# Layer 0's scores and maxima in two row tiles of TensorE, in a two-layer gated cross-attention kernel

## The chip, the cores and the metric

One NeuronCore of a Trainium2 chip runs the whole program. The metric is the device time of one execution in microseconds (us).

The engines are TensorE (PE in the profile; PEld is its weight load), VectorE (DVE), ScalarE (ACT), GpSimd (POOL) and SyncE (SP). Here every DMA is issued by SP, from one queue in the order of the program.

## The reference

Sixteen batches, each of 56 query rows and 1,500 context rows of width 128, go through two layers. A layer is a gated cross-attention (16 heads of 8) and a gated feed-forward with 8 experts, of which each row uses 2.

```python
x = x + tanh(g_xattn[0]) * xattn0(layernorm(x), ctx, ctx, ...)        # no mask
x = x + tanh(g_ffn[0])   * moe0(layernorm(x), ...)                     # E=8, F=512, gelu
x = x + tanh(g_xattn[1]) * xattn1(layernorm(x), ctx, ctx, mask, ...)   # mask on the context rows
x = x + tanh(g_ffn[1])   * moe1(layernorm(x), ...)                     # E=8, F=64, and a shared expert
# xattn: softmax(q k^T / sqrt(8)) v for each head, then the output projection
```

## The kernel before

**Steps.** Work goes by steps `s`. Step `s` has the maxima of batch `n = s` (0 to 15 are layer 0, 16 to 31 are layer 1), the scores and exponentials of the batch before, and the key projection of the batch after. The feed-forward of two batches at a time follows some steps behind: an odd step ends the attention of a pair and begins its experts, the next even step has the rest of the first products and the gelu, and the odd step after that the last second products.

**Sub-steps.** A step has 12 sub-steps `kt`. Each has two maxima on TensorE (`max_scores`, L1010, into `pMX`, 500 columns each), each reduced by VectorE (L920, L925), and two score halves (`score_half`, L972, into `pST`, four matmuls each), each followed by an exponential on ScalarE (L678). Even sub-steps weigh the values of two tiles as well (`weigh`, L993). Key projections (L1115) come at kt 2, 4 and 6, value projections (L1124) at 8, 9 and 10, and small uses of the banks `pFY` and `pFH` at fixed sub-steps (`fy_uses`, `fh_uses`).

**Operands.** Heads go in 8 pairs. An operand for one pair in `kop`, `qmax` or `qexp` has 48 rows of split fp16 parts (`3 * PR`), then 56 mask rows, then 2 shift rows that carry the row maximum `ct`. So a maximum contracts 104 rows and a score 106 in both layers, though in layer 0 the mask rows hold zeros. `pMX` and `pST` have two banks each: a maximum waits for the reduction two maxima back, a score half for the exponential two halves back.

**The SP queue.** DMAs copy keys and queries from SBUF to SBUF into the operands. In a step SP issues, in this order: the shift rows of the last batch (L474, `ct`), key chunk 2 of the present batch (three copies, L462), `qexp` (L486), the context `C` (L493), chunk 0 of the next batch (after the scores have freed it), `qmax` of the next batch (six copies, L508), chunk 1, and in the first steps a few loads of weights (`late_loads`). The first maximum of a step waits for that batch's `qmax`, the score half of tile 0 (kt 3) for the `ct` copy.

**The gelu.** It stands in ScalarE's order at sub-step 8 of even steps, behind the second exponential, with a table load on both sides (L715, L678). The second products `y0` and `y1` (L1082) stand at kt 10 of TensorE's order and wait for it:

```python
                    if experts:
                        small("y0")
                        if has_m(s):
                            max_scores(st, MAXES_PER_KT * kt + 1)
                        small("y1")
                    score_half(st, kt, 0)
```

Of the kernel before, what the change touches and what calls it, by code (L numbers as in the profile page):

```python
# [44 lines left out]
ROWS = SHIFT0 + 2  # L45
RING = 4
# [63 lines left out]
def layer_of(n):  # L110
    return n // B
# [101 lines left out]
def b_total(n):  # L213

    return 48 * min(n + 1, B) + 64 * max(0, n + 1 - B)
# [22 lines left out]
def build(nc, x, ctxT, mask, wpack, bqrow, bcast, wo, bvc, w1_0, w2_0, b2_0, w1_1, w2_1, b2_1, ws2, bs1, out):  # L238
    with ExitStack() as ctx:
# [53 lines left out]
        pick = P[0:S, 0, 0:H * S // 2].bitcast(F16).rearrange("s (h q) -> s h q", h=H)  # L293
        maskin = sb("maskin", [T, S2], I32)
        maskop = sb("maskop", [T, S2], F16)
        shift_rows = maskin[0:1, :].bitcast(F16).rearrange("a (i n) -> a i n", i=2)
# [15 lines left out]
        cc = sb("cc", [T, 2, PAIRS], F16)  # L312
# [4 lines left out]
        XF0, XF = sb("XF0", [T, D]), sb("XF", [T, D])  # L317
# [86 lines left out]
        def _(sp):  # L404
            sp.dma_start(W[:, :], wpack).then_inc(w_in, 16)
            sp.dma_start(bq_row[:, :], bqrow).then_inc(w_in, 16)
            sp.dma_start(bc[:, :], bcast.partition_broadcast(128)).then_inc(w_in, 16)
            sp.dma_start(C[:, :], ctxT[0]).then_inc(c_in, 16)
            sp.dma_start(X[:, :].rearrange("t (g d) -> t g d", g=G),
                         x.rearrange("(g t) d -> t g d", g=G)).then_inc(x_in, 16)  # L410
            sp.wait_ge(init_v, 1)
            sp.wait_ge(init_p, 5)
            for b in range(2):
                sp.dma_start(kop[MASK0:SHIFT0, b, :, :],
                             maskop[0:S, :].unsqueeze(1).broadcast_to([S, PAIRS, S2])).then_inc(init_dma, 16)
                for i in range(2):
                    sp.dma_start(kop[SHIFT0 + i:SHIFT0 + i + 1, b, :, :],
                                 shift_rows[:, i:i + 1, :].broadcast_to([1, PAIRS, S2])).then_inc(init_dma, 16)
                sp.dma_start(qmax[MASK0:SHIFT0, b, :, :, :],
                             pick[:, :, :].rearrange("s (p j) q -> s p j q", j=2)).then_inc(init_dma, 16)  # L420

            def late_loads(s):
# [8 lines left out]
                if s == 1:  # L431
# [5 lines left out]
                    sp.wait_ge(init_dma, 128)  # L437
# [10 lines left out]
            def key_chunk(st, ahead, c):  # L448
# [12 lines left out]
                for row, part in ((0, khi), (PR, klo), (2 * PR, khi)):  # L461
                    sp.dma_start(kop[row:row + PR, dst, :, cols], part[:, cols]).then_inc(kop_in[c], 16)  # L462
                if n >= B:
                    half = S * (n % 2)
                    sp.dma_start(kop[MASK0:SHIFT0, dst, :, cols],
                                 maskop[half:half + S, cols].unsqueeze(1).broadcast_to([S, PAIRS, CW])
                                 ).then_inc(kop_in[c], 16)

            def step(st):
                s = st.s  # L470
                if has_m(s - 1):
                    sp.wait_ge(fy_free, st.at(lambda s: upto(fy_uses, s, "ct", True)))
                    apart(sp)
                    sp.dma_start(qexp[SHIFT0:ROWS, (s - 1) % 2, :, :, :].rearrange("r p j q -> r (p j q)"),  # L474
                                 ct[:, :]).then_inc(shift_in, 16)
                if has_k(s - 1):
                    key_chunk(st, 0, 2)
                if has_m(s):
                    if s == 0:
                        sp.wait_ge(init_dma, 128)  # L480
                    sp.wait_ge(qmax_in, st.at(lambda s: 96 * (s + 1)))
# [4 lines left out]
                    sp.dma_start(qexp[0:SHIFT0, s % 2, :, :, :], qmax[0:SHIFT0, s % 2, :, :, :]).then_inc(qexp_in[s % 2], 16)  # L486
                if s <= NB - 3:
                    if s == -1:
                        sp.wait_ge(init_c, 2 * LAYERS + CH)
# [4 lines left out]
                if has_k(s):  # L494
# [5 lines left out]
                    if s >= 1:  # L500
                        sp.wait_ge(mx_ready, st.at(lambda s: NMAX * s))
                        apart(sp)
                        sp.wait_ge(qexp_in[(s - 1) % 2], st.at(lambda s: 16 * ((s - 1) // 2 + 1)))
                        apart(sp)
                    half = S * ((s + 1) % 2)
                    for row, part in ((0, qhi), (PR, qhi), (2 * PR, qlo)):
                        for j in range(2):
                            sp.dma_start(qmax[row + HD * j:row + HD * (j + 1), (s + 1) % 2, :, j, :],  # L508
                                         part[64 * j:64 * (j + 1), half:half + S]).then_inc(qmax_in, 16)
# [19 lines left out]
        def _(pool):  # L529
            nc.gpsimd.memset(shift_rows[:, 0, :], -BIG).then_inc(init_p, 1)  # L530
# [682 lines left out]
```

## Time and profile before

| | before |
|---|---|
| median of 3 runs | 1040.72 us (1039.66 to 1044.62) |
| the profiled execution: time, span | 1040.23 us, 1038.1 us |
| granted TensorE clock, mean | 0.981 |
| busy: PE, DVE, ACT, POOL | 922.5 us (89%), 723.0 us (70%), 586.2 us (56%), 525.0 us (51%) |

The span runs from the first to the last instruction; the profiled time has 2.1 us more around it. PE's busy time counts overlapping matmuls once, and the end of a matmul is modelled, so it is the distance from one start to the next that tells what a matmul costs.

### The profile page before, as it was taken

Reading aid. Unit: us, or ns where it says so; the run is one execution under the profiler, and the core shown is the slowest. Engines: PE = TensorE matmul, PEld = TensorE weight load, DVE = VectorE, ACT = ScalarE, POOL = GpSimd, SP = SyncE. Lnnn points to the kernel's source line nnn. Section 1 sums busy time; section 2 is a strip of 40 time slices with the busy share of each in tenths; the row PEclk is TensorE's granted clock in tenths of the full one; section 3 lists DMA queues with packets and bytes.
Section 4 is the critical chain, followed back from the end, with each engine's and each line's share of the span. In section 5 each row is a group of like instructions: output and inputs, shape, how many; then the busy total and the mean of one; then the engine's idle time right before and its main releaser. Section 6 shows DMA issues by size and latency. Waiting matters only on the chain.

```text
span 1038.1 us, 32346 instructions
## 1 busy us (share of the span) xinstructions
PE 922.5 (89%) x13088; PEld 675.9 (65%) x13088; DVE 723.0 (70%) x1531; ACT 586.2 (56%) x1060; POOL 525.0 (51%) x667
## 2 busy tenths in 40 slices
PE   2487899999999999999999999999999999999974
PEld 0154577777777777777777777666666666666753
DVE  3376576785767768586785867878787878787722
ACT  1044556556565565656547565665757575757560
POOL 5353445543546335453446565665657576672202
PEclk9998899999999999999999999999999999999995
DMA  8735653333323333233465646767676767665200
GB/s 181 133 90 137 145 126 72 72 83 69 63 55 85 70 77 76 37 81 70 95 137 88 143 110 132 162 123 156 124 152 122 145 130 146 137 137 97 52 2 18
DMA packets 95215, 107.24 MB, mean 103 GB/s; under 512 B 22394, under 2 KB 86972, under 8 KB 95068
## 3 DMA queue, kind: packets, MB, share of 16 engines
q1 hardware_dynamic: 95068, 105.19, 49.0%
q8 instruction: 103, 1.69, 0.8%
q14 instruction: 44, 0.36, 0.1%
HBM read 35.89 MB, written 0.46 MB: 35 GB/s over the span
## 4 chain that ended last, share of the span: by engine, by line
PE 66%; DVE 16%; ACT 9%; issue 5%; SPq 2%; DMA 1%; POOL 0%; POOLq 0%; ACTq 0%; DVEq 0%
PE pO L993 13%; PE pMX L1010 12%; PE pST L972 12%; PE pKV L1124 6%; PE pFY L1082 6%; PE pKV L1115 5%; PE pFH L1150 5%; DVE mx L925 4%; DVE mx L920 4%; ACT P L678 3%; DVE rden L839 3%; PE pFY L1047 2%; ACT HR L715 1%; PE pFY L1086 1%; ACT V L696 1%
## 5 line engine op out<-in xcount | busy, mean ns | idle before, releaser
L678 ACT ACTIVATE P<-pST 125x448 f32<-125x448 f32 x768 | 396.1, 542 | 349.9 <-PE pST L972 344.3
L925 DVE TENSOR_REDUCE mx<-pMX 112x1 f32<-112x500 f32 x384 | 258.4, 673 | 172.3 <-PE pMX L1010 172.1
L1010 PE MATMUL pMX<-kop,qmax 104*112 104x500 f16 x768 | 293.1, 392 | 44.7 <-DMA qmax<-qlo 18.5
L972 PE MATMUL pST<-qexp,kop 106*128 106x112 f16 (+1 forms) x3072 | 280.2, 214 | 19.9 <-ACT P L678 9.3
L972 PEld LDWEIGHTS pST<-qexp,kop 106*128 106x128 f16 (+1 forms) x3072 | 209.9, 102 | 127.1 <-issue 42.9
L920 DVE TENSOR_REDUCE mx<-pMX 112x1 f32<-112x500 f32 x384 | 255.8, 666 | 42.8 <-PE pMX L1010 41.9
L993 PE MATMUL pO<-P,V 125*17 125x112 f32 x6144 | 186.0, 262 | 0.0
L993 PEld LDWEIGHTS pO<-P,V 125*17 125x17 f32 x6144 | 136.8, 98 | 46.2 <-issue 36.3
L1010 PEld LDWEIGHTS pMX<-kop,qmax 104*112 104x112 f16 x768 | 99.0, 132 | 93.1 <-issue 21.7
L563 POOL CAST khi<-kfull 128x500 f16<-128x500 f32 x96 | 57.7, 601 | 193.0 <-ACT kfull L691 192.8
L565 POOL TENSOR_TENSOR klo<-kfull,khi 128x500 f16<-128x500 f32 x96 | 109.0, 1135 | 7.8
L654 POOL TENSOR_TENSOR Clo<-C,Chi 128x500 f16<-128x500 f32 x93 | 105.8, 1138 | 7.5
L691 ACT ACTIVATE kfull<-pKV,W 128x500 f32<-128x500 f32 x96 | 65.0, 677 | 49.2 <-PE pKV L1115 41.1
L652 POOL CAST Chi<-C 128x500 f16<-128x500 f32 x93 | 56.6, 608 | 54.9 <-PE pKV L1124 43.8
L610 POOL TENSOR_TENSOR OM<-OM,rden 128x224 f32<-128x224 f32 x32 | 21.1, 658 | 119.6 <-DVE rden L839 119.6
L1150 PE MATMUL pFH<-xnfT,w1a 128*128 128x112 f32 x512 | 71.6, 283 | 0.0
L1124 PE MATMUL pKV<-Whi,Chi 128*128 128x128 f16 (+1 forms) x384 | 70.9, 222 | 0.7
L1082 PE MATMUL pFY<-w2a,HR 128*112 128x128 f32 x512 | 62.4, 275 | 9.4 <-ACT HR L715 9.4
L1124 PE MATMUL pKV<-Whi,Clo 128*128 128x128 f16 (+1 forms) x384 | 70.4, 221 | 0.0
L1124 PE MATMUL pKV<-Wlo,Chi 128*128 128x128 f16 (+1 forms) x384 | 70.3, 221 | 0.0
L1082 PEld LDWEIGHTS pFY<-w2a,HR 128*112 128x112 f32 x512 | 58.3, 177 | 11.5 <-issue 11.2
L696 ACT ACTIVATE V<-pKV 125x512 f32<-125x512 f32 x96 | 57.3, 597 | 14.5 <-PE pKV L1124 5.6
(144 smaller groups left out, 1089.6 us busy)
## 6 DMA issues: line engine op xcount, KB each, us to landing
C<-in_ctxT SPq DMA_DIRECT2D x32, 750.0 KB, 6.2
kop<-khi SPq DMA_DIRECT2D x192, 125.0 KB
kop<-maskop SPq DMA_DIRECT2D x48, 437.5 KB
kop<-klo SPq DMA_DIRECT2D x96, 125.0 KB
qexp<-qmax SPq DMA_DIRECT2D x32, 182.0 KB
maskin<-in_mask SPq DMA_DIRECT2D x8, 656.2 KB, 6.2
kop<-maskop SPq DMA_DIRECT2D x2, 1312.5 KB
qmax<-qhi SPq DMA_DIRECT2D x128, 7.0 KB
```

Source lines behind the costliest of these rows:

```text
L565: nc.gpsimd.tensor_tensor(klo[:, cols], kfull[:, c, :], khi[:, cols], ALU.subtract).then_inc(klo_done, 1)
L654: nc.gpsimd.tensor_tensor(Clo[:, s % 2, cols], C[:, cols], Chi[:, s % 2, cols], ALU.subtract).then_inc(ctx_split, 1)
L678: nc.scalar.activation(P[0:KP, slot, h * 4 * T:(h + 1) * 4 * T], pST[0:KP, h, 0:4 * T], ACT.Exp, scale=EXP_SCALE).then_inc(exp_done, 1)
L696: nc.scalar.activation(V[0:KP, s % 2, 4 * c:4 * c + 4, :, 0:PR].rearrange("k t p i -> k (t p) i"), pKV[0:KP, :].rearrange("k (m i) -> k m ...
L920: nc.vector.tensor_reduce(mx[:, s % 2, m // PAIRS, m % PAIRS:m % PAIRS + 1], pMX[0:T, 0, 0:CW], AX.X, ALU.max).then_inc(max_done, 1)
L925: nc.vector.tensor_reduce(mx[:, s % 2, m // PAIRS, m % PAIRS:m % PAIRS + 1], pMX[0:T, 1, 0:CW], AX.X, ALU.max).then_inc(max_done, 1)
L972: mm = nc.tensor.matmul(pST[0:cols, h, i * T:(i + 1) * T], kop[0:ROWS, b, p, tile * KP:tile * KP + cols], qexp[0:ROWS, b, p, :, :].rearran ...
L993: mm = nc.tensor.matmul(pO[32 * g:32 * g + VW, r * T:(r + 1) * T], V[0:KP, b, tile, p, :], P[0:KP, tile % RING, p * T:(p + 1) * T], start= ...
L1010: nc.tensor.matmul(pMX[0:T, m % 2, 0:CW], qmax[0:SHIFT0, st.s % 2, p, :, :].rearrange("r j q -> r (j q)"), kop[0:SHIFT0, st.s % 2, p, c * ...
L1082: mm = nc.tensor.matmul(o, HR[:, F0C * e + c, :], w2a[:, e, c, :], start=(c == 0), stop=(c == F0C - 1))
L1124: mm = nc.tensor.matmul(pKV[0:rows, i * D:(i + 1) * D], x_[:, s % 2, cols], m[:, l, 1, :], start=(k == 0), stop=(k == 2))
L1150: mm = nc.tensor.matmul(pFH[:, c * T:(c + 1) * T], w1a[:, e, c * 128:(c + 1) * 128], xnfT[:, :], start=True, stop=True)
```

## The change

In layer 0 the zero mask rows are dropped, so that an operand has 48 rows, or 50 with the shift rows. Pairs 0 to 3 stand from row 0 and pairs 4 to 7 from row 64 of the same tensors. Each matmul of L1010 and L972 then uses a tile of 64 rows of the array, and TensorE's order in a layer-0 sub-step becomes: a maximum of the upper tile, a score half of the lower one, a maximum of the lower, a score half of the upper, and then `weigh` and the projection. Layer 1 keeps its operands and its order, save at kt 10 of even steps.

```diff
+SHIFT0_L0 = 3 * PR
+ROWS_L0 = SHIFT0_L0 + 2
+HALF = 64
...
             def max_scores(st, m):
...
+                if layer_of(n) == 0:
+                    h = 1 - m % 2
+                    rows, slot = slice(HALF * h, HALF * h + SHIFT0_L0), i // 2
+                else:
+                    rows, slot = slice(0, SHIFT0), i
...
                 for kt in range(KT):
+                    m0 = MAXES_PER_KT * kt
+                    together = has_m(s) and layer_of(s) == 0
...
                     if experts:
+                        if has_m(s):
+                            max_scores(st, m0)
+                        weigh(st, kt)
+                        project(kt)
                         small("y0")
                         if has_m(s):
-                            max_scores(st, MAXES_PER_KT * kt + 1)
+                            max_scores(st, m0 + 1)
                         small("y1")
-                    score_half(st, kt, 0)
+                        score_half(st, kt, 0)
+                        score_half(st, kt, 1)
+                    elif together:
+                        for h in range(2):
+                            max_scores(st, m0 + h)
+                            score_half(st, kt, h)
+                        weigh(st, kt)
+                        project(kt)
```

The copies into the operands are split by tile: a key chunk of layer 0 takes six copies instead of three, `qmax` twelve instead of six, `qexp` and `ct` two each instead of one. At the start the copies that filled the mask rows go; the mask and shift rows of layer 1 are filled when it opens.

```diff
                 for row, part in ((0, khi), (PR, klo), (2 * PR, khi)):
-                    sp.dma_start(kop[row:row + PR, dst, :, cols], part[:, cols]).then_inc(kop_in[c], 16)
+                    if n < B:
+                        for h in range(2):
+                            at = HALF * h + row
+                            sp.dma_start(kop[at:at + PR, dst, 0:HP, cols], part[HALF * h:HALF * (h + 1), cols]
+                                         ).then_inc(kop_in[c], 16)
...
-            sp.wait_ge(init_p, 5)
+            sp.wait_ge(init_p, 2)
             for b in range(2):
-                sp.dma_start(kop[MASK0:SHIFT0, b, :, :],
-                             maskop[0:S, :].unsqueeze(1).broadcast_to([S, PAIRS, S2])).then_inc(init_dma, 16)
...
-                sp.dma_start(qmax[MASK0:SHIFT0, b, :, :, :],
-                             pick[:, :, :].rearrange("s (p j) q -> s p j q", j=2)).then_inc(init_dma, 16)
```

On ScalarE the gelu moves from sub-step 8 to 9. In layer 0 a projection is taken out of its bank (`evacuate`) behind both exponentials of its sub-step, and at kt 10 of even steps ahead of both:

```diff
                 for kt in range(KT):
-                    exps(st, kt, 0)
+                    side_by_side = has_m(s) and layer_of(s) == 0
+                    if has_f(s) and kt == 10:
+                        evacuate(kt)
+                    exps(st, kt, 0)
+                    if not side_by_side and not (has_f(s) and kt == 10):
+                        evacuate(kt)
                     exps(st, kt, 1)
+                    if side_by_side and not (has_f(s) and kt == 10):
+                        evacuate(kt)
...
-                    if kt == 8 and has_f(s):
+                    if kt == 9 and has_f(s):
```

**TensorE, sub-steps 3 and 4 of an odd step in layer 0, before** (`pFY<-w2a,HR` is the second product y3 of kt 2, `pO` is `weigh`, `pKV` a key projection):

```order
L1082 MATMUL pFY<-w2a,HR 112x128 x8
L1010 MATMUL pMX<-kop,qmax 112x500
L972 MATMUL pST<-qexp,kop 128x112 x4
L1010 MATMUL pMX<-kop,qmax 112x500
L972 MATMUL pST<-qexp,kop 128x112 x4
L1010 MATMUL pMX<-kop,qmax 112x500
L993 MATMUL pO<-P,V 17x112 x16
L972 MATMUL pST<-qexp,kop 128x112 x4
L1115 MATMUL pKV<-Chi,Whi 128x500
L1115 MATMUL pKV<-Clo,Whi 128x500
L1115 MATMUL pKV<-Chi,Wlo 128x500
```

The same place in the changed kernel:

```order
L1204 MATMUL pFY<-w2a,HR 112x128 x8
L1109 MATMUL pMX<-kop,qmax 112x500
L1067 MATMUL pST<-qexp,kop 128x112 x4
L1109 MATMUL pMX<-kop,qmax 112x500
L1067 MATMUL pST<-qexp,kop 128x112 x4
L1109 MATMUL pMX<-kop,qmax 112x500
L1067 MATMUL pST<-qexp,kop 128x112 x4
L1109 MATMUL pMX<-kop,qmax 112x500
L1067 MATMUL pST<-qexp,kop 128x112 x4
L1088 MATMUL pO<-P,V 17x112 x16
L1141 MATMUL pKV<-Chi,Whi 128x500
```

Both maxima and both score halves of a sub-step now stand next to each other, ahead of `weigh` and the projection.

**SP, the end of step 1, before** (chunk 0, `qmax`, chunk 1, the loads of that step, the shift rows):

```order
L462 DMA kop<-khi 16x8x500 [waits klo_done,st_ready]
L462 DMA kop<-klo 16x8x500
L462 DMA kop<-khi 16x8x500
L508 DMA qmax<-qhi 8x8x56 [waits fh_free,mx_ready,qexp_in0]
L508 DMA qmax<-qhi 8x8x56 x3
L508 DMA qmax<-qlo 8x8x56 x2
```

The same place in the changed kernel:

```order
L489 DMA kop<-khi 16x4x500 [waits klo_done,st_ready]
L489 DMA kop<-khi 16x4x500
L489 DMA kop<-klo 16x4x500 x2
L489 DMA kop<-khi 16x4x500 x2
L560 DMA qmax<-qhi 8x4x56 [waits fh_free,mx_ready,qexp_in0]
L560 DMA qmax<-qhi 8x4x56 x7
L560 DMA qmax<-qlo 8x4x56 x4
```

Nine copies have become eighteen, each of half the size, ahead of chunk 1, the loads and the `ct` copy in the same queue.

## Rows read from the trace of the kernel before

**Rows 1.** Stretches: start:end, length; busy PE, PEld, DVE, ACT, POOL; clock; DMA share; GB/s.

```profile
38.10:154.30 116.20, 98.96 (x1189) 63.94 (x1189) 80.98 (x166) 52.04 (x98) 50.79 (x66) 0.94 0.56 123
154.30:525.40 371.10, 353.18 (x5086) 275.93 (x5086) 267.61 (x555) 220.74 (x385) 178.58 (x235) 1.00 0.35 74
```

**Rows 2.** The chain that ended last: start, us, what.

```profile
90.47 4.05 issue
...
119.11 3.46 issue
```

**Rows 3.** Timeline of PE (start, us, ...): first maxima of steps 11, 12, sub-step 9, step 13.

```profile
368.55 0.38 PE L1010 MATMUL pMX<-kop,qmax 104*112 104x500 f16 x1
...
398.78 0.38 PE L1010 MATMUL pMX<-kop,qmax 104*112 104x500 f16 x1
...
421.73 0.38 PE L1010 MATMUL pMX<-kop,qmax 104*112 104x500 f16 x1
...
431.85 0.38 PE L1010 MATMUL pMX<-kop,qmax 104*112 104x500 f16 x1
```

**Rows 4.** Timeline of ACT, the gelu of step 10.

```profile
358.72 0.54 ACT L678 ACTIVATE P<-pST 125x448 f32<-125x448 f32 x1
359.27 1.28 ACT L715 ACT_TABLE_LOAD   x1
360.57 3.28 ACT L715 ACTIVATE HR<-HR 128x1792 f32<-128x1792 f32 x2
363.87 1.28 ACT L678 ACT_TABLE_LOAD   x1
```

**Rows 5.** Timeline of PE, step 5: maxima and halves back to back, then `weigh`.

```profile
201.34 0.38 PE L1010 MATMUL pMX<-kop,qmax 104*112 104x500 f16 x1
201.56 0.36 PE L972 MATMUL pST<-qexp,kop 106*128 106x112 f16 x4
201.75 0.38 PE L1010 MATMUL pMX<-kop,qmax 104*112 104x500 f16 x1
...
203.40 0.38 PE L1010 MATMUL pMX<-kop,qmax 104*112 104x500 f16 x1
203.71 0.96 PE L993 MATMUL pO<-P,V 125*17 125x112 f32 x32
204.60 0.37 PE L972 MATMUL pST<-qexp,kop 106*128 106x112 f16 x4
```

**Rows 6.** Timeline of all engines, step 11, around sub-step 3.

```profile
377.92 0.69 DVE L867 TENSOR_TENSOR ysc<-pFY,gate 112x512 f32<-112x512 f32 x1 [1.34 <-PE pFY L1082]
...
378.53 0.67 DVE L920 TENSOR_REDUCE mx<-pMX 112x1 f32<-112x500 f32 x1
379.11 0.67 DVE L925 TENSOR_REDUCE mx<-pMX 112x1 f32<-112x500 f32 x1
...
379.34 0.39 PE L1010 MATMUL pMX<-kop,qmax 104*112 104x500 f16 x1 [0.64 <-DVE mx L920]
```

**Rows 7.** Timeline of SP (SPq), the start.

```profile
6.79 1.01 SPq L414 DMA_DIRECT2D kop<-maskop  x1
...
27.52 0.68 SPq L462 DMA_DIRECT2D kop<-khi  x1
```

**Rows 8.** Timeline of POOL, low part of the first key chunk.

```profile
16.15 1.13 POOL L565 TENSOR_TENSOR klo<-kfull,khi 128x500 f16<-128x500 f32 x1
```

**Rows 9.** Timeline of PE, the first maxima.

```profile
38.11 1.08 PE L1010 MATMUL pMX<-kop,qmax 104*112 104x500 f16 x2 [18.54 <-DMA qmax<-qlo]
```

**Rows 10.** Timeline of SP, step 2: chunk 0, qmax, a load of weights.

```profile
103.45 0.55 SPq L462 DMA_DIRECT2D kop<-khi  x1
104.05 0.59 SPq L462 DMA_DIRECT2D kop<-klo  x1
...
109.17 1.26 SPq L508 DMA_DIRECT2D qmax<-qlo  x2
...
113.31 0.60 SPq L440 DMA_DIRECT2D w1a<-in_w  x1
```

More of the change, by code:

```diff
@@ L210, in pool_links, with opens_layer, b_total, q_total @@
     return n
-def b_total(n):
-    return 48 * min(n + 1, B) + 64 * max(0, n + 1 - B)
+def opens_layer(n):
+    return n in (B, B + 1)
+def b_total(n, c):
+    return sum(96 if layer_of(t) == 0 else 80 if opens_layer(t) and c == CH - 1 else 64 for t in range(n + 1))
+def q_total(n):
+    return sum(192 if layer_of(t) == 0 else 112 if opens_layer(t) else 96 for t in range(n + 1))
+def qexp_total(n):
+    return sum(32 if layer_of(t) == 0 else 16 for t in range(n % 2, n + 1, 2))
 class Step:
@@ L507, in step @@
                         for j in range(2):
-                            sp.dma_start(qmax[row + HD * j:row + HD * (j + 1), (s + 1) % 2, :, j, :],
-                                         part[64 * j:64 * (j + 1), half:half + S]).then_inc(qmax_in, 16)
+                            if s + 1 < B:
+                                for h in range(2):
+                                    at, of = HALF * h + row + HD * j, HALF * h + HALF // 2 * j
+                                    sp.dma_start(qmax[at:at + HD, (s + 1) % 2, 0:HP, j, :],
+                                                 part[of:of + HALF // 2, half:half + S]).then_inc(qmax_in, 16)
+                            else:
+                                sp.dma_start(qmax[row + HD * j:row + HD * (j + 1), (s + 1) % 2, :, j, :],
+                                             part[64 * j:64 * (j + 1), half:half + S]).then_inc(qmax_in, 16)
+                    if opens_layer(s + 1):
+                        sp.dma_start(qmax[MASK0:SHIFT0, (s + 1) % 2, :, :, :].rearrange("s p j q -> s (p j) q"),
+                                     pick[:, :].unsqueeze(1).broadcast_to([S, H, S])).then_inc(qmax_in, 16)
                 if s >= B - 1 and has_mask(s + 1):
@@ L682, in step, with evacuate @@
                 s = st.s
-                for kt in range(KT):
-                    exps(st, kt, 0)
+                def evacuate(kt):
                     for use in [u[1] for u in kv_uses(s) if u[0] == kt]:
@@ L989, in weigh @@
                     for r in range(2):
-                        pe.wait_ge(exp_done, st.at(lambda s: 2 * (KT * (s - back) + tile) + r + 1))
+                        pe.wait_ge(exp_done, 2 * (KT * (st.s - back) + tile) + r + 1)
                         for g in range(4):
@@ L1127, in step @@
-                    if has_m(s) and not experts:
-                        max_scores(st, MAXES_PER_KT * kt + 1)
-                    score_half(st, kt, 1)
+                        score_half(st, kt, 0)
+                        score_half(st, kt, 1)
+                    elif together:
+                        for h in range(2):
+                            max_scores(st, m0 + h)
+                            score_half(st, kt, h)
+                        weigh(st, kt)
+                        project(kt)
+                    else:
+                        if apart_ and not late:
+                            max_scores(st, m0)
+                        weigh(st, kt)
+                        score_half(st, kt, 0)
+                        if apart_ and late:
+                            max_scores(st, m0)
+                        project(kt)
+                        if apart_:
+                            max_scores(st, m0 + 1)
+                        score_half(st, kt, 1)
```

262 lines of the change are left out of this document (155 added, 107 removed).

## The prediction

> **What bounds the kernel now.** I read the busy time by stretches first, then the timeline of each engine in one pair of layer-0 steps, then the queue of SP at the start. Between 154 and 525 us, layer 0 in its steady state, TensorE is busy 353 of 371 us at full clock, with VectorE at 268 and ScalarE at 221 [rows 1]. From 38 to 154 us it is busy 99 of 116 [rows 1], and two of the holes there are single waits of 4.05 and 3.46 us at sub-step 3 [rows 2]. Steps alternate: from one first maximum to the next, odd step 11 takes 30.2 us and even step 12 takes 33.1, so a pair takes 63.3 [rows 3]. So TensorE bounds the odd steps, and the even ones save for the gelu: the gelu with its table loads holds ScalarE for 5.9 us, from 359.27 to 365.15 [rows 4].
>
> **Part 1, the pair in two row tiles.** A maximum starts, its score half follows 0.22 us later, the next maximum 0.19 after that: 0.41 us for each half of a sub-step, 0.82 for both [rows 5]. If tiles overlap, a half costs the longer of the two, 0.21, and a step saves 12 x 0.40 = 4.8 us. If they don't, it saves nothing. No row shows two row tiles at work; the nearest are the column tiles of `weigh`, 32 matmuls in 0.89 us, 0.028 each against some 0.05 for each score matmul of about as many columns [rows 5]. Tiles do overlap there, so I take the overlap.
>
> The Trainium skill, TensorEngine Tiling (Array Packing), Key Properties, says that different tiles execute in parallel, but that changing the tiling mode drains TensorE. By its first sentence alone the saving would be the whole 4.8 us; the second speaks against the change, and the trace has its size:
>
> Switch of tile shape: a maximum is followed after 0.31 us by `weigh` instead of 0.22, so 0.09 for a switch, and the same on the way back [rows 5]. In layer 0 the old order switches twice in each sub-step with `weigh`; the new one switches once more there, and twice in odd sub-steps that have small uses. That is some 12 more, 12 x 0.09 = 1.1 us a step.
>
> **Part 2, what comes to bound in place of TensorE.** On its own work alone an odd step would take 30.2 - 4.8 + 1.1 = 26.5 us. VectorE is next. Two reductions take about 0.6 us each when back to back, and a maximum starts 0.14 us after the reduction that frees its bank [rows 6]. Sub-step 3 shows it: `ysc` 0.6 (until the next start), reduction 0.6, handoff 0.14, so the next maximum waits about 1.4 us from the end of y3 [rows 6]. TensorE has 0.82 us of work for that now and 0.42 afterwards, so 0.4 of the wait of 0.64 is added. Its second maximum, which stood behind `weigh`, now stands ahead of it and waits another 0.4 us for the second reduction; the score half, `weigh` and the projection queue behind it. I went through the 12 sub-steps of both steps like this, each by the later of TensorE's work and VectorE's two reductions with what lies ahead of them. TensorE waits 2.7 us in an odd step (sub-steps 3, 4, 5, 6, 8, and 0, whose halves wait for late exponentials), which gives 29.2 us. In an even step sub-steps 0 to 8 took 22.95 us [rows 3]; 9 x 0.40 comes off, 0.9 for switches and 2.1 of waits (expert additions and the reciprocal on VectorE) come on: 22.35.
>
> Sub-steps 9 to 11 took 10.1 us [rows 3]. The gelu block started right behind the exponential of sub-step 8. Now two exponentials (0.54 each) and a value evacuation stand ahead of it, and TensorE's shorter pairs only bring up the start of these; I get the block 1.3 us later against sub-step 9. The third value projection fills part of the wait before y0, and from y0 to the end the stretch is 0.5 us shorter. So 10.9, and an even step stays at 33.2. A pair takes 62.4 instead of 63.3. Layer 0 has about 5.9 such pairs from 154 us on: -5.4 us. Bounds: -23 if VectorE's waits vanish (26.5 us is then too low, since SP bounds it, below: about 28, and 31.5 for the even step), +4 if a half costs 0.25 instead of 0.21.
>
> **Part 3, the start.** SP copies mask and shift rows from 6.79 us and comes to the first key chunk only at 27.52 [rows 7], though its low part is ready at 17.28 [rows 8]; the first maximum is at 38.11 [rows 9]. These copies go. Four small copies take their place and end before 17 us. Then come six key copies and twelve of `qmax`. A copy takes 0.60 to 0.64 us of SP with its gap, for a key copy of 125 KB and for a `qmax` copy of 7 KB alike [rows 10], so I take it that halves cost as much as wholes. That gives 17.8 + 6 x 0.64 + 12 x 0.65 = 29.5, some 1.2 for landing, and the first maximum at 30.7: -7.4 us.
>
> **Part 4, SP's queue in the steps with loads.** Now each step issues 17 copies more, 11 us of issue. In steady state they fit (11.5 us of issue become about 22 in a step of 30), only just: in an odd step, chunk 0 is released at sub-step 6, 16.0 us in, and 18 copies and the landing, 12.9 us, end at 29.2, where the next step begins. In steps 0 to 3 more loads stand behind chunk 1, and the `ct` copy behind them. In step 2 chunk 0 starts at 103.45 and the load `w1a` ends at 113.91 [rows 10]; the score half that needs `ct` starts at 122.57 [rows 2], 8.7 us after that load is issued. What is late is what was late before: sub-step 3 of the next step. Step by step, with each wait as above: the eight small loads of step 0 push `ct` to 61.6 (step 1 is then 3.2 us ahead of before at sub-step 3, no longer 7.4), step 2 comes out even with before, step 3 is 4.5 us late and step 4, behind `w2a`, 7.4. The cover of the added issue is gone exactly where SP didn't wait before. Together, parts 3 and 4: +7.4 us. Bounds: -3 if a half key copy costs 0.47 with its gap (a copy from HBM goes at such rates), +9.
>
> **Part 5, the seam and layer 1.** In step 16 layer-1 maxima are of 128 rows and the scores still of 64, in the old order, so tiles switch about 3 times more per sub-step: 36 x 0.09 = 3.2, some of it under the gelu: +3.0. In steps 16 and 18 the long gelu starts a sub-step later with no shorter pairs: +0.9 each, 1.8. In later even steps the short gelu and the earlier projection cancel: 0 (bounds -3, +3). Mask and `pick` rows when layer 1 opens are two or three copies with a sub-step or more of room: 0.
>
> **Sum**, against the profiled execution's 1040.23: -5.4 + 7.4 + 3.0 + 1.8 = +6.8, so 1047.0. That execution lies 0.5 us under the median of the runs, so little that I leave it: **1047 us**.
>
> **Rivals.**
> - **It is faster: TensorE's saving reaches the end.** VectorE has 104 us free of 371 [rows 1]; if its waits fall into gaps that I count twice, and half copies are issued faster, pairs save up to 3.9 us: -23 - 3 + 4.8 = -21, 1019; half of that waits gives 1030. It decides if an odd step comes under 28.6 us. Against it: each reduction hands on only the bank of two maxima back [rows 6]. Chance 0.32, 1018 to 1035.
> - **Gains and costs cancel.** Parts 3 and 4 at -3 with the rest as forecast gives 1037; at 0, 1040. With halves at a little under 0.6 this is quite possible. Chance 0.2 for within 0.5%.
> - **Row tiles don't overlap**, since a short score matmul behind a long maximum may have to wait for its end. The pair is 0.82 again with 1.1 us of switches on top, and steps grow by up to 1.1 us: about 12 x 1.1 in place of -5.4, so 1061 to 1066. The Trainium skill, TensorE: Matmul & The Clock Gate, Part 3, has matmuls that start and end strictly in program order, and packs of equal length that overlap; no run here shows unequal ones yet. Chance 0.13.
> - **The forecast**, slower by SP's queue and the waits on VectorE: 0.35, own range 1041 to 1055.
>
> The measurement can't tell less than about 0.5% (5.2 us) from no change. The chances of slower are those of the forecast (most of it) and of no overlap: 0.46; same 0.22; faster 0.32. The range 1020 to 1062 leaves 0.2 out at its ends.
>
> **What would show it.** Right: a score half starts within 0.02 us of its maximum; pairs of steps near 62.4 us with TensorE waiting on VectorE at sub-steps 3 to 6; first maximum near 30.7 us; the lead lost by sub-step 3 of step 4, with SP issuing without a pause before it; the even step unchanged, the gelu starting 2.1 us into sub-step 9. Wrong: SP issuing half copies in 0.4 us, a lead kept past step 4, an odd step under 28.6 us, or a pair at 0.8 us.

## The result and the profile after

The changed kernel takes 1087.1 us (median of 4 runs, 1076.4 to 1095.6) against 1042.1 for the kernel before: the ratio is 1.040, with an interval of 1.030 to 1.050. I had forecast 1047 and a range up to 1062, so the direction is right, and the size is not. The profiled execution is the longest of the four and counts as slow: 1095.6 us, a span of 1093.9 and a granted clock of 0.926 instead of 0.981, where the other three had 0.929 to 0.955, so the rows below show what the clock costs at its most.

The stretches of the changed kernel: up to step 4 (30.29 to 154.22), the rest of layer 0, and steps 7 to 9 and a part of step 10 each. Columns as in [rows 1].

```profile
30.29:154.22 123.93, 95.03 (x1066) 56.41 (x1067) 74.75 (x154) 47.86 (x91) 49.14 (x63) 0.78 0.35 96
154.22:563.69 409.47, 358.67 (x5208) 278.42 (x5209) 271.09 (x567) 224.99 (x392) 179.28 (x236) 0.93 0.24 70
260.88:292.40 31.52, 27.21 (x432) 20.70 (x428) 24.36 (x53) 16.59 (x33) 17.39 (x25) 0.98 0.22 67
292.40:332.09 39.69, 35.86 (x442) 28.34 (x442) 21.21 (x43) 20.66 (x33) 11.80 (x15) 0.80 0.17 54
332.09:364.15 32.06, 27.20 (x431) 20.70 (x427) 24.36 (x53) 16.59 (x33) 17.55 (x25) 0.98 0.22 66
...
364.15:376.00 11.85, 11.85 (x116) 9.53 (x117) 5.19 (x10) 3.08 (x7) 0.00 (x0) 0.50 0.16 50
376.00:403.80 27.80, 23.97 (x328) 18.76 (x326) 16.02 (x33) 17.58 (x27) 11.64 (x14) 0.93 0.18 55
```

These two odd steps take 31.5 and 32.1 us instead of 30.2, and steps 8 and 10 take 39.7 and 39.6 instead of 33.1 [rows 3]. They are the worst: the even steps 6 to 14 take 34.3, 39.7, 39.6, 37.0 and 32.7 us, the odd ones 5 to 15 between 29.3 and 32.1. TensorE has less to do in an odd step (27.2 us busy), and yet the step is longer. The first 11.9 us of step 10 run wholly at the lower of the two clock levels (0.50, 1.2 GHz). The end of step 9 shows why, first on SP, then on TensorE.

```profile
348.21 2.37 SPq L489 DMA_DIRECT2D kop<-khi  x2
350.63 1.23 SPq L489 DMA_DIRECT2D kop<-klo  x2
351.90 1.23 SPq L489 DMA_DIRECT2D kop<-khi  x2
353.39 6.76 SPq L560 DMA_DIRECT2D qmax<-qhi  x8
360.20 2.81 SPq L560 DMA_DIRECT2D qmax<-qlo  x4
```

```profile
359.17 0.41 PE L1109 MATMUL pMX<-kop,qmax 48*112 48x500 f16 x1
359.17 0.37 PE L1067 MATMUL pST<-qexp,kop 50*128 50x112 f16 x4
359.38 0.37 PE L1109 MATMUL pMX<-kop,qmax 48*112 48x500 f16 x1
359.42 0.36 PE L1067 MATMUL pST<-qexp,kop 50*128 50x112 f16 x4
359.95 1.15 PE L1270 MATMUL pFH<-xnfT,w1a 128*128 128x112 f32 x8 [0.17 <-DVE HR L879]
364.15 0.66 PE L1109 MATMUL pMX<-kop,qmax 48*112 48x500 f16 x1 [3.06 <-DMA qmax<-qlo]
```

Two things are to be seen. The row tiles work: a score half starts 0.01 us after its maximum, and the next maximum 0.21 later. And the first maximum of step 10 waits 3.06 us for the last `qmax` copy, which SP finished issuing at 363.01. After that wait a maximum takes 0.66 us instead of 0.38: the clock has fallen.

It falls a second time in the same step, at sub-step 10. There the second product y0 waits for the gelu, and the 3.4 us from 397.10 on are at the lower level again:

```profile
396.39 3.09 PE L1204 MATMUL pFY<-w2a,HR 128*112 128x128 f32 x16 [1.77 <-ACT HR L784]
```

```profile
397.10:400.50 3.40, 3.40 (x15) 2.72 (x14) 0.39 (x1) 2.50 (x3) 0.00 (x0) 0.50 0.02 3
```

In the kernel before, y0 waits 1.17 us in each even step and the clock stays up.

The span is 55.8 us longer. By the first maxima of steps 5, 16, 20 and 31 (178.66, 525.40, 652.17 and 956.34 before; 196.58, 563.69, 696.97 and 1005.81 now), it comes apart so:

| stretch | measured | forecast |
|---|---|---|
| first maximum | -7.8 | -7.4 |
| steps 0 to 4 | +25.7 | +14.8 |
| steps 5 to 15 | +20.4 | -5.4 |
| steps 16 to 19 | +6.5 | +4.8 |
| steps 20 to 30 | +4.7 | 0 |
| the rest | +6.3 | 0 |

The rest is the tail, in which the clock fell some 43 us after the first maximum of step 31, instead of 56. This can't be put down to the change: from that maximum to the end it is 81.8 us in the kernel before and in two of the experiments below (before_split, tiles_nine_best), and between 82 and 88 in the others, whatever their edit. What decides it was not tried.

### The profile page after: what moved, and what is told of

Its sections match the earlier page's. It is cut to its first block, busy times and chain, and to the rows that moved or that the text cites. A ratio compares the mean times of both kernels' runs of the same rounds, so it can differ in the third digit from the quotient of the medians.

```text
span 1093.9 us, 32642 instructions
## 1 busy us (share of the span) xinstructions
PE 937.4 (86%) x13088; PEld 677.0 (62%) x13088; DVE 723.3 (66%) x1537; ACT 586.7 (54%) x1060; POOL 518.8 (47%) x666
## 4 chain that ended last, share of the span: by engine, by line
PE 54%; DVE 20%; SPq 10%; issue 7%; ACT 6%; DMA 2%; POOL 1%; POOLq 0%; DVEq 0%
DVE mx L973 11%; PE pO L1088 11%; PE pST L1067 8%; PE pMX L1109 8%; PE pFY L1204 6%; SPq L560 6%; PE pFH L1270 5%; PE pKV L1141 5%; PE pKV L1150 4%; SPq L489 4%; DVE rden L915 2%; PE pFY L1208 2%; ACT P L736 2%; ACT HR L784 1%; DVE HR L879 1%
## 5 line engine op out<-in xcount | busy, mean ns | idle before, releaser
L973 DVE TENSOR_REDUCE mx<-pMX 112x1 f32<-112x500 f32 x768 | 487.9, 668 | 204.6 <-PE pMX L1109 201.6
L736 ACT ACTIVATE P<-pST 125x448 f32<-125x448 f32 x768 | 389.0, 542 | 340.9 <-PE pST L1067 335.1
L1109 PE MATMUL pMX<-kop,qmax 48*112 48x500 f16 (+1 forms) x768 | 291.2, 419 | 63.2 <-DVE mx L973 27.7
L1067 PE MATMUL pST<-qexp,kop 50*128 50x112 f16 (+2 forms) x3072 | 273.1, 219 | 25.1 <-issue 14.7
L1067 PEld LDWEIGHTS pST<-qexp,kop 50*128 50x128 f16 (+2 forms) x3072 | 189.0, 103 | 93.3 <-issue 40.0
L1088 PE MATMUL pO<-P,V 125*17 125x112 f32 x6144 | 197.0, 272 | 0.0
L1109 PEld LDWEIGHTS pMX<-kop,qmax 48*112 48x112 f16 (+1 forms) x768 | 99.2, 132 | 140.9 <-DVE mx L973 55.2
L750 ACT ACTIVATE kfull<-pKV,bkp 128x500 f32<-128x500 f32 x48 | 32.5, 677 | 84.6 <-PE pKV L1141 84.6
L1270 PEld LDWEIGHTS pFH<-xnfT,w1a 128*128 128x128 f32 x512 | 70.6, 209 | 10.7 <-DVE HR L879 6.1
L755 ACT ACTIVATE V<-pKV 125x512 f32<-125x512 f32 x96 | 57.1, 594 | 34.1 <-PE pKV L1150 29.2
L879 DVE TENSOR_TENSOR HR<-pFH,W 128x448 f32<-128x448 f32 x64 | 39.4, 616 | 36.4 <-PE pFH L1270 35.5
## 6 DMA issues: line engine op xcount, KB each, us to landing
kop<-khi SPq DMA_DIRECT2D x192, 62.5 KB
kop<-klo SPq DMA_DIRECT2D x96, 62.5 KB
```

Source lines behind the costliest of these rows:

```text
L736: nc.scalar.activation(P[0:KP, slot, h * 4 * T:(h + 1) * 4 * T], pST[0:KP, h, 0:4 * T], ACT.Exp, scale=EXP_SCALE).then_inc(exp_done, 1)
L973: nc.vector.tensor_reduce(mx[:, s % 2, c, p:p + 1], pMX[0:T, m % 2, 0:CW], AX.X, ALU.max).then_inc(max_done, 1)
L1067: mm = nc.tensor.matmul(pST[0:keys.stop - keys.start, h, i * T:(i + 1) * T], kop[rows, b, slot, keys], qexp[rows, b, slot, :, :].rearrange ...
L1088: mm = nc.tensor.matmul(pO[32 * g:32 * g + VW, r * T:(r + 1) * T], V[0:KP, b, tile, p, :], P[0:KP, tile % RING, p * T:(p + 1) * T], start= ...
L1109: nc.tensor.matmul(pMX[0:T, m % 2, 0:CW], qmax[rows, b, slot, :, :].rearrange("r j q -> r (j q)"), kop[rows, b, slot, c * CW:(c + 1) * CW] ...
L1270: mm = nc.tensor.matmul(pFH[:, c * T:(c + 1) * T], w1a[:, e, c * 128:(c + 1) * 128], xnfT[:, :], start=True, stop=True)
```

## The experiments

The kernel before was run beside each on the same chip: 1043.1 us in the first set, 1043.8, 1043.3 and 1042.6 in the later ones.

**1. nine_copies.** A copy may write to rows with a stride, so one copy can fill both row tiles if an operand's rows stand 4 apart. The heads are ordered to suit. Each tile's operands then have 64 rows, zeros among them, and the first loads take fewer copies too. Layer 1 of this kernel keeps stale entries of layer 0 in rows that should be zero, so its values are not the reference's; its operations are the same.

```diff
-                        for h in range(2):
-                            at = HALF * h + row
-                            sp.dma_start(kop[at:at + PR, dst, 0:HP, cols], part[HALF * h:HALF * (h + 1), cols]
-                                         ).then_inc(kop_in[c], 16)
+                        sp.dma_start(kop[row // PR:128:4, dst, 0:HP, cols], part[:, cols]).then_inc(kop_in[c], 16)
```

> The changed kernel with its row tiles and its orders, but with as many copies in layer 0 as before (3 for a key chunk, 6 for qmax, 1 for qexp and for ct): the rows of an operand are spread over both tiles with a stride of 4 rows, so that one copy fills both. Theory A (SP's queue is what costs, and a TensorE that waits for qmax at the end of an odd step then runs the next step at the lower clock): odd steps of layer 0 near 28 us, even ones near 32, the clock at 1.0 from step 5 on, and a time of 1005 to 1022 us, below the kernel before. Theory B (row tiles cost by themselves: changes of tile shape and waits on VectorE's reductions): a pair of steps stays above 63 us and the time above 1060.

Measured: 1030.3 us (1029.3 to 1030.6), ratio 0.989 (0.985 to 0.992). Steps 9 and 10:

```profile
283.67:312.61 28.94, 27.13 (x431) 20.70 (x427) 22.16 (x49) 16.60 (x33) 14.91 (x23) 1.00 0.28 87
312.61:346.14 33.53, 28.90 (x443) 22.67 (x442) 23.13 (x49) 20.66 (x33) 14.32 (x17) 1.00 0.16 52
```

The same tiles and the same orders, at full clock, in 28.9 and 33.5 us: a pair in 62.5. Theory A holds, though the time is 8 us above my range for it, since I had put the pair near 60. Theory B's 63 us is missed by little. So the tiles and orders give 0.8 us a pair when the copies are as few as before, and the changed kernel, with its eighteen copies, takes 56.8 us more in all.

**2. before_split.** The other side: the old kernel with the copies alone.

```diff
-                    sp.dma_start(kop[row:row + PR, dst, :, cols], part[:, cols]).then_inc(kop_in[c], 16)
+                        for h in range(2):
+                            sp.dma_start(kop[row + 8 * h:row + 8 * h + 8, dst, :, cols],
+                                         part[64 * h:64 * (h + 1), cols]).then_inc(kop_in[c], 16)
```

> The kernel before, with each key copy and each qmax copy of layer 0 made in two halves (eighteen for nine), nothing else changed: no row tiles, the mask rows and the old start stay. Theory A: qmax lands some 32 us into an odd step instead of 29 or less, so odd steps take 31.5 to 33 us instead of 30.2, part of the even ones start at the lower clock, and the time is 1060 to 1085 us. Theory B: steps stay at 30.2 and 33.1 from step 5 on, and the time is under 1050.

Measured: 1080.6 us (1075.5 to 1083.6), ratio 1.036 (1.032 to 1.041). Steps 0 to 4, step 9, step 10; then the first maximum of step 10:

```profile
40.47:208.09 167.62, 132.55 (x1508) 87.82 (x1508) 97.29 (x197) 69.44 (x124) 65.24 (x78) 0.86 0.46 99
339.75:371.56 31.81, 29.61 (x427) 22.73 (x427) 22.83 (x49) 15.87 (x31) 16.77 (x25) 1.00 0.35 69
371.56:404.66 33.10, 30.94 (x442) 24.48 (x442) 22.37 (x44) 20.65 (x33) 11.85 (x15) 1.00 0.35 67
```

```profile
371.56 0.42 PE L1026 MATMUL pMX<-kop,qmax 104*112 104x500 f16 x1 [1.39 <-DMA qmax<-qlo]
```

Steps 0 to 4 take 167.6 us, 27.1 more than before, as in the changed kernel (+25.7). Odd steps take 31.8 us, with the same wait for `qmax`. Here that wait is 1.39 us, and from step 5 to 15 the clock stays at 1.00. Theory A holds in the odd steps and the time, but not in its lower clock for even steps. The copies alone cost 37.5 us without row tiles. With them (changed kernel against nine_copies) they cost 56.8: its odd steps have less work of their own, so the waits are longer and the clock falls.

**3. filled_wait.** Useless matmuls in the wait.

```diff
                 if m == 0:
+                    if n >= 6 and n % 2 == 0 and layer_of(n) == 0:
+                        pe.wait_ge(max_done, NMAX * n - 1)
+                        for _ in range(12):
+                            nc.tensor.matmul(pMX[0:T, 0, 0:CW], Whi[:, 0, 0, 0:T],
...
                     pe.wait_ge(qmax_in, q_total(n))
```

> The changed kernel with twelve matmuls of 500 columns on constants put ahead of the first maximum of steps 6, 8, 10, 12 and 14, into the bank that this maximum overwrites, ahead of its wait for qmax: some 2.5 us of work of no use, inside a wait of about 3 us. Theory A (the wait lets the clock fall to its lower level, which costs 4 to 6.6 us in each of these steps): even steps near 33 us, 15 to 25 us less than the changed kernel. Rival (the clock falls for another reason, such as the many short waits before, or the fall costs nothing): no gain, or 2 us lost for each of the five.

Measured: 1078.5 us (1073.4 to 1081.9), ratio 1.035 (1.030 to 1.040). Around the start of step 10, and the stretches of steps 9 and 10:

```profile
354.93 2.69 PE L1102 MATMUL pMX<-Whi 128*112 128x500 f16 x12
357.55 0.41 PE L1115 MATMUL pMX<-kop,qmax 48*112 48x500 f16 x1
```

```profile
326.08:357.55 31.47, 29.66 (x443) 22.16 (x440) 24.37 (x53) 16.60 (x33) 17.36 (x25) 1.00 0.22 71
357.55:390.20 32.65, 28.65 (x442) 22.66 (x442) 21.04 (x43) 20.65 (x33) 11.86 (x15) 1.00 0.20 62
```

Step 10 takes 32.65 us instead of 39.64, for 2.6 us of work of no use in a wait that was there anyway. Of these 7.0 us, 5.4 are in sub-steps 0 to 8, which now run at full clock (21.4 us instead of 26.9). The other 1.6 are at sub-step 10: the second fall, which the filling doesn't touch, is absent from this step but comes in steps 8 and 14 of the same run, which take 34.3 and 34.2 us. From step 5 to 15 the profiled execution saves 13.9 us. The medians differ by 8.6 only, less than the 15 I expected. The changed kernel's profiled execution was its longest, at a clock of 0.926, where its shorter runs had 0.951 and 0.955.

**4. no_mask_rows.** The shorter operands alone.

```diff
+                rows = slice(0, SHIFT0_L0) if layer_of(st.s) == 0 else slice(0, SHIFT0)
                 nc.tensor.matmul(pMX[0:T, m % 2, 0:CW],
-                                 qmax[0:SHIFT0, st.s % 2, p, :, :].rearrange("r j q -> r (j q)"),
+                                 qmax[rows, st.s % 2, p, :, :].rearrange("r j q -> r (j q)"),
```

> The kernel before without the mask rows in layer 0 (operands of 48 and 50 rows), all eight pairs in one tile as before, whole copies, the old orders. It has the shorter start alone. If the queue ate the lead of the start in the changed kernel (theory A), here the lead of about 7 us is kept: 1032 to 1037 us. If the shorter start itself is lost in the steps with loads of weights, whatever the copies (rival): 1039 to 1044.

Measured: 1087.8 us (1080.3 to 1100.0), ratio 1.042 (1.033 to 1.050). Both expectations failed. The first maximum is early (24.25), but the steps are longer. Step 11, and matmuls in step 13:

```profile
397.48:430.58 33.10, 32.52 (x430) 23.06 (x427) 22.52 (x49) 16.71 (x33) 17.29 (x26) 1.00 0.36 74
```

```profile
443.73 0.37 PE L1133 MATMUL pKV<-Chi,Wlo 128*128 128x500 f16 x1
444.04 0.41 PE L1028 MATMUL pMX<-kop,qmax 48*112 48x500 f16 x1
444.29 0.36 PE L991 MATMUL pST<-qexp,kop 50*128 50x112 f16 x4
444.58 1.15 PE L1168 MATMUL pFH<-xnfT,w1a 128*128 128x112 f32 x8
```

A maximum starts 0.31 us after the last matmul of a projection, where 500 columns need 0.21; the first products start 0.29 after a score half that needs 0.19. These are the 0.09 of a change of tile shape that I had read at `weigh` [rows 5]. An operand of 48 rows costs a change at each meeting with a projection or product of 128 rows. Counted in the trace, step 11 has 46 changes of shape, and 20 in the kernel before. These 26 more make 2.4 of the 2.9 us by which the step is longer. Part of the rest is that a score half follows its maximum after 0.255 us here (median), and after 0.215 before.

**5. no_mask_66_rows.** The same with 16 rows of zeros behind, which take the matmuls back to the whole array.

```diff
+FULL_L0 = ROWS_L0 + 16
...
-                rows = slice(0, SHIFT0_L0) if layer_of(st.s) == 0 else slice(0, SHIFT0)
+                rows = slice(0, FULL_L0) if layer_of(st.s) == 0 else slice(0, SHIFT0)
```

> no_mask_rows with operands of 66 rows (48 parts, 2 shift rows, 16 rows of zeros that are filled once), so that each maximum and score again uses the whole array of 128 rows, not a tile of 64. If the change of tile shape is what cost no_mask_rows 2 to 3 us a step (0.093 us at each change between a maximum or score and a projection, a first product or a second product): steps at 30.2 and 33.1 again from step 5 on. If the number of rows also decides when TensorE's clock rises in the first steps: with 66 rows it rises earlier than with 48 (there at some 83 us), and the lead of 13 us at the first maximum is kept: 1025 to 1031. Rival (the short operands themselves are what costs, by their rows): steps stay at 33.1 and 35.3, and the time above 1060.

Measured: 1045.9 us (1044.1 to 1050.1), ratio 1.003 (1.000 to 1.007). Steps 11 and 12 are those of before again [rows 3], so it is the shape, and not the number of rows as such, that costs:

```profile
369.41:399.62 30.21, 29.39 (x431) 22.68 (x428) 22.16 (x48) 16.59 (x33) 15.96 (x24) 1.00 0.37 81
399.62:432.67 33.05, 30.88 (x444) 24.36 (x442) 23.64 (x49) 20.65 (x33) 13.29 (x17) 1.00 0.27 57
```

The early start is not kept, though. The first maximum is at 32.43, and step 1 takes 29.3 us against 22.1 before. TensorE reaches the higher clock at 50.3 us, loses it again after 6.8 us and has it back at 77.6:

```profile
50.30:57.10 6.80, 4.60 (x27) 2.03 (x26) 5.99 (x13) 1.19 (x2) 3.58 (x5) 1.00 0.06 12
57.10:77.60 20.50, 20.36 (x154) 12.69 (x152) 10.38 (x21) 8.62 (x15) 7.43 (x11) 0.50 0.38 85
```

The kernel before reaches it at 56.8 us, where its value projections' matmuls begin to start 0.055 us apart instead of 0.107, and keeps it to 90.9.

**6. nine_copies_2.** Adds the clearing that nine_copies lacked.

```diff
+                    if opens_layer(s + 1):
+                        sp.dma_start(qmax[0:SHIFT0_L0, (s + 1) % 2, :, :, :].rearrange("s p j q -> s (p j) q"),
+                                     zero[:, :].unsqueeze(1).broadcast_to([SHIFT0_L0, H, S])).then_inc(cleared, 16)
+                        sp.wait_ge(cleared, 16 * (s + 2 - B))
```

> nine_copies, with the queries' rows cleared when layer 1 opens (one copy and one wait on SP in each of two steps), so that layer 1 computes the reference again. 1030 us within 2 us, if those two copies are hidden, as they should be: SP has some 10 us to spare in those steps.

Measured: 1042.3 us (1039.1 to 1046.4), ratio 0.999 (0.995 to 1.003): 12 us lost, not 2. The chain in step 15:

```profile
493.07 6.61 DMA qmax<-zero
...
503.83 3.14 DMA qmax<-pick
```

A copy of 768 pieces of 112 bytes takes 6.6 us to land, with the queue behind it. Step 15 takes 33.3 us instead of 29.3, and step 16, at a clock of 0.84, 42.6 instead of 36.6: its first maximum waits 3.78 us for `pick`, the last copy into `qmax`, as the changed kernel's even steps wait for theirs. Steps 10, 14 and 18 take 1.6 to 1.7 us more each. In them the clock falls for 3.4 us behind the wait of y0 for the gelu (1.77 us, in step 18 1.92), which has the same length in nine_copies, where it doesn't fall.

**7. old_gelu_layer1** and **8. old_gelu_all** put the gelu back, and with it the order at sub-step 10 (TensorE's products ahead of the third value projection), which the diff leaves out.

```diff
-                    if kt == 9 and has_f(s):
+                    if kt == (8 if early_gelu(s) else 9) and has_f(s):
```

> nine_copies_2 with the gelu back at sub-step 8 and sub-step 10 in the old order (products ahead of the third value projection) from step 16 on. If the later gelu is what shifts layer 1, so that in its odd steps VectorE's second operation on `cc` starts while GpSimd's `Clo` runs and takes 1.03 us instead of 0.17 (theory A): odd steps of layer 1 back at 28.1 us instead of 28.9, steps 16 and 18 each 0.9 shorter, 5 to 7 us less in all, about 1024. Rival (the shift has another source, in the order of the copies of ct for instance): odd steps stay at 28.9, about 2 us less.

> The same in every even step, layer 0 too. If the later gelu costs more than it gives in layer 0 (my working: 0.5 us saved, 1.3 us of delay), even steps 6 to 14 take 32.7 us instead of 33.5, 4 to 5 us less than old_gelu_layer1. Rival (the wait of y0 was worth filling, since the gelu cannot start earlier than its exponentials allow): 0 to 3 us more.

Measured: 1039.4 us (1036.8 to 1040.5), ratio 0.9960 (0.9925 to 0.9995), and 1033.5 us (1031.1 to 1036.2), ratio 0.990 (0.987 to 0.994). Step 21 of the first, and steps 11 and 12 of the second:

```profile
674.11:702.23 28.12, 27.20 (x404) 19.80 (x400) 22.22 (x48) 17.56 (x35) 18.55 (x29) 1.00 0.70 153
```

```profile
346.29:375.01 28.72, 26.98 (x431) 20.75 (x429) 22.03 (x49) 16.45 (x33) 15.50 (x24) 1.00 0.27 88
375.01:407.87 32.86, 28.85 (x443) 22.66 (x442) 23.32 (x49) 20.84 (x33) 13.65 (x17) 1.00 0.17 54
```

Odd steps of layer 1 are back at 28.1 us, and step 18 at 33.15 from 35.67. The median gains 2.9 us and not the 5 to 7 expected. Step 17 begins at the same 549.65 us as in nine_copies_2, since its first maximum waits for the copy of `pick` (now 2.04 us, there 0.12), and behind that wait the clock is at 0.50 for 6.8 us, so that the step takes 34.1 us instead of 31.1. In layer 0 the old place is worth 0.66 us in an even step and 0.2 in an odd one, and 2.3 in steps 10 and 14, where the clock doesn't fall at y0 any more: it waits 1.02 us there. The second run is 5.9 us below the first, where 4 to 5 were expected.

**9. tiles_nine_best.** Row tiles, nine copies, the old gelu and no clearing: a stride of 8 gives each row the same head of its pair in both layers.

```diff
-                                sp.dma_start(qmax[row + HD * j:row + HD * (j + 1), (s + 1) % 2, :, j, :],
+                                sp.dma_start(qmax[row // PR + 4 * j:HALF:8, (s + 1) % 2, :, j, :],
```

> Row tiles with nine copies a step and the old gelu, in a layout that needs no clearing at the seam: in both layers an operand's rows stand 8 apart, so that a row belongs to the same head of its pair in layer 0 and in layer 1; layer 1 has its mask rows from row 64 on. From old_gelu_all (1033.5) the seam's delay should go: step 15 at 28.9 to 29.3 us instead of 33.0, step 16 at 36 instead of 43. So 1022 to 1026 us. Rival (layer 1's operands of 120 and 122 rows, or copies of one row in 4, cost something in layer 1): odd and even steps of layer 1 above 28.1 and 27.3, and no gain over 1030.

Measured: **1013.3 us** (1009.6 to 1017.5), ratio 0.972 (0.968 to 0.975), the fastest of all. Steps 11 and 12, then step 21:

```profile
340.01:368.74 28.73, 26.99 (x431) 20.75 (x429) 22.04 (x49) 16.46 (x33) 15.54 (x24) 1.00 0.28 88
368.74:401.62 32.88, 28.85 (x443) 22.66 (x442) 23.36 (x49) 20.84 (x33) 13.68 (x17) 1.00 0.17 54
649.26:677.39 28.13, 27.22 (x403) 19.81 (x400) 22.23 (x48) 17.55 (x35) 18.61 (x29) 1.00 0.59 154
```

It gains 9 us more than expected: steps 15 to 17 take 95.6 us against 110.1 in old_gelu_all, and steps 0 to 4 take 131.0 against 135.6. Of the 29.8 us of span gained on before, 23.5 are there by step 5 (13.9 at the first maximum), and 9.5 come from steps 5 to 15; the seam gives 2.8 back.

**10. tiles_apart.** Its order undone.

```diff
-                    side_by_side = has_m(s) and layer_of(s) == 0
+                    side_by_side = False
...
-                    together = has_m(s) and layer_of(s) == 0
-                    apart_ = has_m(s) and layer_of(s) == 1
+                    together = False
+                    apart_ = has_m(s)
```

> tiles_nine_best with the order of TensorE and ScalarE in layer 0 as before the change: maxima and score halves no longer side by side, both tiles still used. If it is the order that makes a pair of tiles overlap, a step gains little from the tiles and pays for the changes of tile shape, as no_mask_rows did: odd steps 31 to 33 us, even 34 to 35, and 1060 to 1085. Rival (a score half overlaps with the maximum before it in any order, since they stand next to each other there too, and only the second half of the gain is lost): 29.5 to 30.5 and 33 to 34, 1028 to 1045.

Measured: 1048.4 us (1046.1 to 1057.0), ratio 1.007 (1.004 to 1.010). Steps 11 and 12:

```profile
364.57:395.86 31.29, 29.28 (x431) 21.19 (x428) 22.15 (x49) 16.32 (x33) 16.58 (x25) 1.00 0.25 81
395.86:430.87 35.01, 30.98 (x443) 23.03 (x442) 24.03 (x49) 20.63 (x33) 12.62 (x16) 1.00 0.16 51
```

A pair takes 66.3 us against 61.6. The steps are as the first theory has them, the time lies between the two, and the order is worth 4.7 us a pair. The pair has 88 changes of shape here and 62 in tiles_nine_best, by the traces. These 26 make 2.4 us, and the rest should be overlap that is lost where the order parts a maximum from its score half; where they still stand next to each other, they still start together (371.78 us).

**11. changed_old_gelu.** The changed kernel with the same edit as 8 alone.

> The changed kernel itself, with eighteen copies, and only the gelu back at sub-step 8 and the third value projection behind the products. If the two prices add (theory A): the same gain as between nine_copies_2 and old_gelu_all in layer 1, some 7 us (odd steps at 28.1, steps 16 and 18 shorter), and little in layer 0, where SP's queue decides when an even step begins: 1076 to 1082 us. If the gelu is what lets SP fall behind in layer 0 (rival): even steps of layer 0 at 33 us throughout and a time under 1065.

Measured: 1067.8 us (1054.9 to 1072.5), ratio 1.020 (1.015 to 1.025). 19 us are gained, where I had expected 5 to 11. Steps 8 and 10:

```profile
288.47:324.61 36.14, 32.93 (x442) 26.31 (x442) 21.42 (x43) 20.84 (x33) 11.36 (x15) 0.87 0.20 59
...
355.90:389.45 33.55, 30.16 (x441) 23.87 (x442) 21.36 (x43) 20.83 (x33) 11.27 (x15) 0.95 0.21 63
```

Neither theory fits: the time lies between their ranges. Steps 8 and 10 take 36.1 and 33.6 us instead of 39.7 and 39.6, a comparison with the longest run of the changed kernel. Of the difference 2.2 us in each are in sub-steps 9 to 11 (10.56 us instead of 12.80), where y0 waits 1.02 us and not 1.77 and the clock doesn't fall. Both steps still start below full clock, but for less time. Why an earlier gelu shortens that stretch is open.

## Why the prediction was wrong

**Parts 1 and 2, the tiles: right.** With the copies out of the way (nine_copies) an odd step takes 28.9 us and an even one 33.5, 62.5 a pair; the forecast was 29.2, 33.2 and 62.4. That it comes so close in the odd step is partly luck. I had added 2.7 us of waits to work shortened by 3.7; step 9 there idles for 1.8 us in all, 0.9 of it at sub-step 3, and TensorE's busy time falls by 2.3 only (27.1 from 29.4). The changes of tile shape are 0.09 us each, as read, and 10 more in an odd step where I had some 12. What I had not seen is that short operands bring them without row tiles too (no_mask_rows), and that without the side-by-side order they outweigh the tiles (tiles_apart). The Trainium skill, TensorEngine Tiling (Array Packing), Key Properties, has both sides: tiles run in parallel, and a change of mode drains TensorE. The trace agrees on the first, with 0.01 us from a maximum to its score half. For the second it shows a cost of 0.09 us, and not whether that is a drain. The rival without overlap is out.

**Part 3, the start: right** (-7.8 for -7.4).

**Part 4, SP's queue: the step that failed.** I wrote that in steady state 18 copies and the landing take 12.9 us and "fit, only just", ending at 29.2 us of an odd step. Chunk 0 was released as I had it (16.1 us in), but the first maximum came 15.9 us after it: 5.2 us to the first `qmax` copy and not 3.8, 9.6 until the last is issued and not 7.8, and 1.1 for landing. A half copy of `qmax` takes 0.71 us with its gap, where a whole one takes 0.65 [rows 10], and one copy of `kop` and one of `qmax` took 1.7 and 1.6 us (hence 2.37 for the first two of `kop`). I had no room for an error of 3 us, put the fit at the edge and costed it at nothing. The step ends at 32.1 us and not at 29.2. That the added copies are what costs is shown from both sides: without them the time is 1030.3 us (nine_copies), and with them alone the old kernel takes 1080.6 (before_split).

**What stood nowhere in it: the clock.** I priced TensorE at full speed throughout. Behind the waits for `qmax` of 2.50, 3.06 and 1.88 us before steps 8, 10 and 12 it was at 0.50; behind those of 1.00 and 0.99 before steps 6 and 14 it stayed up. In steps 5 to 15 the changed kernel takes 25.4 us more than nine_copies. The five waits are 9.4 us of it. Sub-steps 0 to 8 of steps 8, 10 and 12 take 26.9, 26.9 and 25.8 us instead of the 21.4 of steps 6 and 14, 15.2 more. (With the falls at sub-step 10, below, that is some 4 us too many, since sub-steps 0 to 8 take 22.3 us in nine_copies.) filled_wait shows that it is this wait, and that it costs more than itself. The Trainium skill, TensorE: Matmul & The Clock Gate, HAM oscillation — how this bites in real kernels, describes a wait for DMA before each group of matmuls, behind which the clock is found lowered. The trace agrees, with 0.50 behind the wait of 3.06 us; the rule was there to be weighed, and I did not make it a rival. In steps 0 to 4 waits and clock come together and were not taken apart: 25.7 us lost for 14.8, and 27.1 in before_split. The lead was gone by the first maximum of step 2 (83.7 us for 81.6), not in step 4.

The gelu's move adds to this, against part 2, where the projection was to fill part of the wait of y0. That wait grew from 1.17 us to 1.77 in layer 0 and to 1.92 in step 18. In steps 6, 8, 10 and 18 of the changed kernel the clock fell behind it for 3.4 us, 1.6 to 1.7 us each. With the same waits it fell in steps 10, 14 and 18 of nine_copies_2 and in none of nine_copies; with the old gelu (waits of 1.02 to 1.17 us) it fell behind none of them.

**Part 5.** The seam's sum was near (6.5 for 4.8), with other terms: 3.4 us in step 16 for 3.9, 0.9 in step 17 for 0, 2.5 in step 18 for 0.9 (1.7 of them by the clock), and -0.3 in step 19. "In later even steps the short gelu and the earlier projection cancel" was right for even steps (27.4 for 27.3), but the odd ones took 28.9 instead of 28.1, which I had not looked at. VectorE and GpSimd of the changed kernel, step 21:

```profile
725.25 0.17 DVE L987 TENSOR_SCALAR cc<-m 112x8 f16<-112x8 f32 x1
725.46 1.03 DVE L988 SCALAR_TENSOR_TENSOR cc<-cc,m 112x8 f16<-112x8 f16 x1
```

```profile
725.34 1.14 POOL L712 TENSOR_TENSOR Clo<-C,Chi 128x500 f16<-128x500 f32 x1
```

The second operation on `cc` took 1.03 us, and ended with `Clo`, in the five odd steps where `Clo` had begun 0.13 us ahead of it. In the others, where it starts 0.02 us before `Clo` or with `Clo` idle, it takes 0.17. The old gelu with its order moves it back (experiment 7). The Trainium skill, SBUF — State Buffer, SBUF: two separate sides, says that a VectorE operation with two SBUF inputs and a GpSimd operation that reads SBUF share ports, which the first to start holds to its end; the rows agree.

## What to carry to other kernels

When an edit makes more transfers out of the same bytes, lay their issue time out against the time from release to need: if it fits only just, take it as a new bound, and look for a layout (here a partition stride) that keeps the count. Price a wait of TensorE with the clock behind it, and look again at every wait that the edit lengthens, if by half a microsecond only. Before operands are made shorter, count how often matmuls of another tile shape stand between them: in this kernel short operands paid only side by side.

## What I had not expected of the hardware

- A score half of four matmuls of 112 columns overlaps fully with a maximum of 500 columns in the other row tile (0.21 us for both), though their lengths differ.
- Half the bytes did not make a copy cheaper for SP: 0.59 us for a key copy of 125 KB or 62 KB, and 0.67 against 0.61 for `qmax`.
- In steps 0 and 1 the granted clock reads 1.00 in the rows of no_mask_rows, while its 500-column matmuls start 0.415 us apart, as at 1.2 GHz. By the spacing of matmuls and the granted clock behind it, TensorE first reaches the higher level at 56.8 us in the kernel before, and keeps it for 34 us. With row tiles and nine copies it is there for 3 to 7 us at 44 to 47 us, falls back, and is there again at 57 (tiles_apart) to 72 us (old_gelu_all). With 66 rows in one tile it is there at 50 and again at 78, and with 48 rows not before 81. What decides it is open; it was not tried alone.
